# Layer 0 attention: q/k channels stored by groups of four heads

## The reference

```
q, k, v = split_heads(x @ Wq + bq), split_heads(x @ Wk + bk), split_heads(x @ Wv + bv)
pos_k = split(rel_embeddings @ Wk + bk)                # 64 positions x 16 heads x 8
scores = (q k^T + take(q pos_k^T, bucket(i - j)) + take(k pos_k^T, bucket(j - i))^T) / sqrt(24)
ctx = softmax(scores) @ v
x += layernorm(ctx @ Wo + bo + xn) + xn @ sign(weight).T + ...
```

## Time and profile before

| | us |
|---|---|
| median of 3 runs | 2037.45 (2034.83 to 2041.1) |
| profiled execution | 2038.12 |
| its span, first to last instruction | 2036.3 |
| PE busy / VectorE / ScalarE / GpSimd | 1878.0 / 1517.2 / 1475.5 / 1200.4 |
| mean granted TensorE clock | 0.966 |

### The profile page before, as it was taken

The page is one execution under the profiler, slowest core; times in us unless marked ns, Lnnn a source line. Parts: engine busy times, 40 slices in busy tenths (PEclk is TensorE's granted clock), DMA queues, the critical chain, the costliest instruction groups (busy, mean ns, idle before and its releaser), DMA issues.

```text
span 2036.3 us, 38730 instructions
## 1 busy us (share of the span) xinstructions
PE 1878.0 (92%) x13494; PEld 1471.1 (72%) x13494; DVE 1517.2 (75%) x3871; ACT 1475.5 (72%) x2979; POOL 1200.4 (59%) x1027
## 2 busy tenths in 40 slices
PE   4899999999999996789998999999999888889998
PEld 3677777777777774554776888888887666668797
DVE  7677777777787874474488888888889777754686
ACT  6788888888888885334466677777776677775675
POOL 3888889798888873365255555555556444447200
PEclk7999999999999999699998999999999899999999
DMA  6999999999999992101000000000010000012001
GB/s 189 334 337 327 326 332 322 316 338 308 342 314 329 323 327 74 72 1 41 1 6 1 1 1 1 1 1 1 1 33 1 1 1 1 1 47 79 12 1 42
DMA packets 72263, 263.98 MB, mean 130 GB/s; under 512 B 10822, under 2 KB 30406, under 8 KB 71558
## 3 DMA queue, kind: packets, MB, share of 16 engines
q1 hardware_dynamic: 71126, 256.53, 36.6%
q10 hardware_dynamic: 944, 4.98, 0.6%
HBM read 140.17 MB, written 121.31 MB: 128 GB/s over the span
## 4 chain that ended last, share of the span: by engine, by line
PE 42%; DVE 7%; ACT 6%; POOL 2%; issue 1%; DVEq 0%; ACTq 0%; POOLq 0%
PE PS L157 10%; PE PS L339 8%; PE PS L161 8%; PE PS L163 8%; PE PS L162 8%; ACT AR L167 3%; ACT L167 2%; DVE AR L185 1%; DVE DR L181 1%; ACT PT L171 1%; DVE PT L181 1%; POOL AR L176 1%; DVE AR L193 1%; DVE AR L176 1%; DVE AR L181 0%
## 5 line engine op out<-in xcount | busy, mean ns | idle before, releaser
L167 ACT ACTIVATE AR<-PS,AR 128x512 f32<-128x512 f32 x1024 | 702.9, 693 | 164.6 <-PE PS L339 69.6
L339 PE MATMUL PS<-ident,AR 128*128 128x128 f32 x3816 | 581.3, 277 | 29.7 <-DVE PT L181 16.1
L339 PEld LDWEIGHTS PS<-ident,AR 128*128 128x128 f32 x3816 | 445.2, 142 | 122.7 <-issue 41.4
L157 PE MATMUL PS<-AR 128*128 128x128 bf16 (+7 forms) x4126 | 472.2, 357 | 38.1 <-DVE AR L1394 14.1
L181 POOL TENSOR_TENSOR AR<-AR 128x512 f32<-128x512 f32 (+7 forms) x325 | 385.1, 1199 | 184.1 <-DVE AR L181 64.2
L207 DVE CUSTOM_DVE_ANT_0 PS<-PS,AR 128x512 f32<-128x512 f32 x512 | 353.3, 695 | 165.9 <-PE PS L587 162.8
L176 POOL TENSOR_SCALAR AR<-AR 128x512 f32<-128x512 f32 (+1 forms) x146 | 255.9, 1754 | 263.8 <-DVE AR L1798 195.7
L157 PEld LDWEIGHTS PS<-AR 128*128 128x128 bf16 (+4 forms) x4126 | 297.7, 131 | 141.7 <-issue 92.1
L171 ACT ACTIVATE AR<-PS 128x512 f32<-128x512 f32 (+3 forms) x596 | 354.6, 597 | 49.9 <-PE PS L157 27.8
L193 DVE TENSOR_REDUCE AR<-PS 128x1 f32<-128x512 f32 x384 | 263.9, 688 | 82.7 <-PE PS L163 76.1
L171 ACT ACTIVATE PT<-PS 128x512 fp32r<-128x512 f32 x320 | 191.4, 598 | 161.9 <-PE PS L339 127.3
(11 more groups left out here) (177 smaller groups left out, 3070.2 us busy)
## 6 DMA issues: line engine op xcount, KB each, us to landing
scr<-AR SPq DMA_DIRECT2D x128, 800.0 KB, 5.2
XN<-scr SPq DMA_DIRECT2D x85, 768.0 KB, 7.1
AR<-scr SPq DMA_DIRECT2D x43, 768.0 KB, 7.2
AR<-qsc SPq DMA_DIRECT2D x96, 192.0 KB
qsc<-AR SPq DMA_DIRECT2D x16, 384.0 KB, 4.4
qsc<-AR SPq DMA_DIRECT2D x16, 256.0 KB, 4.6
AR<-in_wgu SPq DMA_DIRECT2D x16, 256.0 KB, 3.2
qsc<-AR SPq DMA_DIRECT2D x16, 128.0 KB, 4.9
```

Source lines behind the costliest of these rows:

```text
L157: return pe.e.matmul(out, lhsT, rhs, start=start, stop=stop)
L167: return ac.e.activation(out, in_, func, bias=bias, scale=scale, accum_out=accum)
L339: return pe.e.transpose(out, in_, ident[0:k, 0:k])
```

## The change

Channels are ordered by group of four heads first, then channel-in-head, then head in the group: partition p = 32 g + 4 d + h'. The weights' columns, the biases and `mask16` are reordered with it. In each block of `qsc` a group's 32 rows now lie together, 32 KB. The wide reads get a new source pattern, six blocks of eight runs of 4 KB. For `PGO` the four heads of each group must now be picked apart, so its reads run over four dimensions of 1 KB pieces, and the two that covered 24 partitions at once become three each: 12 DMAs instead of 8.

```diff
--- before.py
+++ after.py
@@ -22,7 +22,9 @@
 
 BACK_D = ROW_D - 64
 BACK = BACK_D + FRAME_D[3] + 192
-QSZ = 2 * 16 * 48 * 512 + 16 * 12 * 512
+QPART = 128 * 512
+QFAR = 2 * 6 * QPART
+QSZ = QFAR + 16 * 12 * 512
 SC = float(1.0 / np.sqrt(np.float32(24.0)))
 
 
@@ -74,12 +76,13 @@
     c["iota"] = np.tile(np.arange(64, dtype=np.float32)[None, :], (128, 1))
     c["rev"] = np.tile(np.arange(8, 0, -1).astype(np.float32)[None, :], (128, 1))
     head = i // 8
+    head_by_channel = 4 * (i // 32) + i % 4
     pat = np.zeros((128, 3), np.float32)
     pat[54:57, 0] = 1
     pat[48:51, 1] = 1
     pat[51:54, 2] = 1
     c["pat"] = pat
-    c["mask16"] = (i[:, None] % 16 == i[None, :16]).astype(np.float32)
+    c["mask16"] = (head_by_channel[:, None] == i[None, :16]).astype(np.float32)
     c["bdmask"] = (head[:, None] == head[None, :]).astype(np.float32)
     return c
 
@@ -625,7 +628,7 @@
             norm_tr(pe, 0, 2, 4, 2)
             norm_tr(pe, 0, 3, 4, 3)
             pe.wait_ge(*emptied[number["g0", 0, 0]])
-            pe.wait_ge(pg_r, 8 * 16)
+            pe.wait_ge(pg_r, 12 * 16)
             pe.wait_ge(dv_init, PV_0)
             for n in range(2):
                 g_of(n, 0)
@@ -1055,13 +1058,12 @@
             sp.wait_ge(po_init, PGO_0)
             for k in range(2):
                 for part, first, step, times in PLACES[1 - k]:
-                    for x in range(first, first + step * times, step if step > 1 else times):
-                        n = times if step == 1 else 1
-                        src = bass.AP(pgd.tensor, (2 * part + k) * 128 * 128, [[0, n], [2048, 8], [1, 2048]])
-                        sp.e.dma_start(flat(PGO[8 * x:8 * (x + n), k]), src).then_inc(pg_r, 16)
+                    for x in range(first, first + step * times, step):
+                        src = bass.AP(pgd.tensor, (2 * part + k) * 128 * 128, [[512, 8], [4096, 4], [1, 512]])
+                        sp.e.dma_start(flat(PGO[8 * x:8 * x + 8, k]), src).then_inc(pg_r, 16)
 
             def q_write(b, k):
-                base = b % 2 * QSZ + k * 16 * 48 * 512
+                base = b % 2 * QSZ + k * 6 * QPART
                 sp.wait_ge(sp_p, 6 * b + 2 * k + 2 if b else SPLIT0[k, 1])
                 sp.wait_ge(sp_a, 6 * b + 2 * k + 2 if b else SPLIT0[k, 1])
                 if b >= 2:
@@ -1074,14 +1076,14 @@
                                    flat(PARTS[2][0:64])).then_inc(qw[b % 2], 16)
                     return
                 for part, first, step, times in PLACES[k]:
-                    dst = bass.AP(qsc.tensor, base + first * 8 * 8192, [[512, 128], [step * 8 * 8192, times], [1, 512]])
+                    dst = bass.AP(qsc.tensor, base + first * QPART, [[512, 128], [step * QPART, times], [1, 512]])
                     sp.e.dma_start(dst, bc(PARTS[k][:, part:part + 1, :], [128, times, 512])).then_inc(qw[b % 2], 16)
 
             def rows(G, k):
-                return bass.AP(qsc.tensor, G // 4 % 2 * QSZ + k * 16 * 48 * 512 + G % 4 * 2048, [[8192, 48], [1, 2048]])
+                return bass.AP(qsc.tensor, G // 4 % 2 * QSZ + k * 6 * QPART + G % 4 * 32 * 512, [[QPART, 6], [2048, 8], [1, 2048]])
 
             def far_rows(G, k, n):
-                at = G // 4 % 2 * QSZ + 2 * 16 * 48 * 512 + (32 * (k // 2) + 8 * (G % 4) + k % 2) * 1536
+                at = G // 4 % 2 * QSZ + QFAR + (32 * (k // 2) + 8 * (G % 4) + k % 2) * 1536
                 return bass.AP(qsc.tensor, at, [[512, n], [3072, 4], [1, 512]])
 
             def load_group(G):
@@ -2908,7 +2910,7 @@
     d = constants()
 
     d["x"] = f["L0_attn_hidden_states"].reshape(NT, 128, 128).transpose(1, 0, 2)
-    by_channel = np.arange(128).reshape(16, 8).T.reshape(128)
+    by_channel = np.arange(128).reshape(4, 4, 8).transpose(0, 2, 1).reshape(128)
     d["l0_wq"], d["l0_wk"] = f["L0_attn_Wq"][:, by_channel], f["L0_attn_Wk"][:, by_channel]
     d["l0_wv"], d["l0_wo"] = f["L0_attn_Wv"], f["L0_attn_Wo"]
     d["l0_sw"] = f["L0_ffn_weight"].T
```

## The result

| | before | after |
|---|---|---|
| median of 9 runs | 2037.58 us (2033.82 to 2041.1) | 2045.12 us (2040.38 to 2047.82) |
| ratio, 95% interval | | 1.0036 [1.0027, 1.0045] |
| profiled execution, span | 2038.1, 2036.3 | 2041.8, 2040.0 |
| mean granted TensorE clock | 0.966 | 0.967 |

The change costs 7.5 us, where 17 were forecast: the likeliest case in kind (slower, with six engines on the wide reads), with its price more than twofold too high. The profiled execution is one of the quicker ones of the changed kernel, 3.3 us under its median. So I took the same kernel's profile once more (run e10_after_again, 2049.55 us) and read both.

A forecast was written before the change was run, and what follows sets the result against it. It took PE as nearly full, 590.2 of 600 us busy, with the DMA engines close behind at share 0.94. Loop lateness 16 plus start 1.3 made 17 us, so 2055 us; range 2036 to 2110.

The forecast's parts named there:

- the likeliest case: Layer 0's attention loop: six engines just full from the wide reads, 2055 us, own range 2044 to 2080; chance 0.52.
- What bounds it: Steady loop: PE busy 590.2 of 600 us, DMA share 0.94; two resources close to full.
- Six engines: Wide reads of `qsc`: outer count falls from 48 to 6, so six engines carry 32 KB each per read.
- the rival that the read is still spread over sixteen: Wide reads: each engine has 20.4 us of work per group; shares the chances of 0.10 (faster) and 0.18 (hidden).
- The work of the fullest engine: Per group in the loop: six engines 22.6 us, lowest three 22.9, in a period of 22.9 us.
- The choice of 3.6 us for six engines against 9.8: Wide reads per group on six engines: 3.6 us at 27.3 GB/s taken, 9.8 us at 10.1 GB/s rejected.
- the rival of slow packets: Wide reads: 4 KB packets stay slow, half of them giving 2137 us, a quarter 2089; chance 0.20 with the mild form.
- a third of it: Loop: a third of the lateness of up to 1.7 us reaches PE, 0.5 us per group, 16 us in all.
- The route: Loop: late `scr` transfers meet GpSimd's wait, then reach `least` on VectorE, then the exponential, then PE.
- Bursts: Head issuing a group's two loads: 7.15 us of work against 5.71, so it falls behind and two heads catch up.
- The slow rate: Early wide reads before the change: 161 GB/s at share 1.00, tied to rows 16 KB apart.
- The start: `PGO` reads: 12 DMAs instead of 8 delay the writes of q and k and the first load, costing 1.3 us.

The follow-up runs named there:

- e10_after_again: The changed kernel with no edit, run again for a second profile: 2044.33 us, ratio 1.0037; its profiled execution 2049.55 us.
- e7: Changed kernel with a group's two wide reads of `load_group` issued four steps apart instead of one behind the other: 2050.11 us, ratio 1.0072.
- e12: Changed kernel with the wide reads issued between a head's write and its read of `scr`, instead of behind the read: 2057.17 us, ratio 1.0095.
- e5: Changed kernel with a group's 48 rows in one piece, read over sixteen engines, each `qsc` write split into four: 2044.87 us, ratio 1.0041.
- the probe: Kernel before, plus six stretches of eight 4 KB-row reads after its output's store, varying row spacing and destination partitions: 2106.32 us including these reads.
- e1: Changed kernel with operand rows ordered channel-in-head first, so wide reads have outer count 8 and use eight engines: 2041.26 us, ratio 1.0024.

## Why the prediction was right or wrong

**What bounds it.** Right. PE remains the bound, busy for 97 to 98% of the steady stretch, and easing the DMA engines brings nothing: no run beats the kernel before.

**Six engines.** Right, and the rival that the read is still spread over sixteen fell with the share of 0.36 and 129 GB/s for a wide read alone. In the steady stretch the GB/s stay while the share falls by 0.03 to 0.04. The rule on engine counts that I took from the Trainium skill, "DMA: Bandwidth & Descriptors", section "Why a DMA increments its semaphore by 16 and not by 1", agrees with the traces here for three and six.

**The work of the fullest engine.** Right where it can be tested. By the same sum eight engines carry 2.7 us of wide reads per group, near the 2.5 taken for before, and the loop stays at 721 us. Three carry 7.2; the sum gives (26.5 - 22.9) x 32 = 115 us, and the loop grew by 104. The choice of 3.6 us for six engines against 9.8 is borne out, and the rival of slow packets in both its forms fell with it.

**The step that failed** is "I let a third of it through to PE, 0.5 us per group: 32 x 0.5 = 16 us". In the two profiles the loop grew by 2.0 and 9.2 us, 0.06 and 0.29 us per group; by the medians (7.5 - 1.0) / 32 = 0.2. The third was no measurement but a guess between none and all. It was set at a place where hardly any lateness goes through: GpSimd's waits grew by half and VectorE saw 0.6 us more. That 41 of 105 heads have a wait there only shows that GpSimd is early; the 0.2 us of VectorE in the earlier trace rows show that none of it was passed on, not how much room is left. I took the cover as used up. It held another 28 us of GpSimd's waits, but for one place at a batch's `tail`. Nor is the price a fraction of every group's lateness: what PE lost, it lost in a few long waits.

**The route.** Wrong in the main. As far as the waits show it, most of the lateness that reaches PE goes through the write of `scr`. It lands at 6.1 instead of 5.2 us, VectorE waits for its buffer 9.5 and 13.3 us instead of 0, and in the second profile PE waits 6.3 us more for VectorE. In the first profile nothing of the 9.5 reaches PE as a wait for VectorE between 100 and 700 us, so for that execution's 2.0 us the route is not shown; the predicted route has 0.59 us of it. Three engines enlarge that route to 83.5 and 51.8 us, while the wait for GpSimd stays at 6.1. In the prediction writes stood beside reads as landing up to 1.7 us later, but I asked for the readers' waits only. Who waits for a write was counted for SyncE alone; before the change no compute engine did. e7 and e12 limit this: with reads a little later still the predicted route becomes the dear one, and it opens at the heads that share GpSimd with a batch's `tail`.

**Bursts.** Not shown. The working let a head with two loads fall behind and two heads catch up; taking the loads apart eased the waits for writes, but late reads met GpSimd's `tail` and the changed kernel became slower. How much the burst itself costs stays open.

**The slow rate.** The number 161 GB/s was read rightly, its cause was not. That "the 16 KB spacing that goes with the slow rate is gone" is refuted as a reason by e5 (170 GB/s with touching rows) and by the probe (154 against 161). It is the 48 neighbouring partitions of the destination, and the change left these alone. The share of 1.00 there was no measure of work: the sixteen engines are counted busy while they are held back. That six engines draw no more than this rate is why they lose nothing on a wide read alone; it was the second of the two reasons given for 3.6 us, and it alone carries. The Trainium skill, "DMA: Bandwidth & Descriptors", section "Latency and other measured facts", ties slow copies to large powers of two in the row spacing; no run here shows that at 16 KB, and the use I made of it as a direction was wrong.

**The start.** The size was right (1.0 to 1.3 us), the working not. 12 issues took 4.10 us and not 5.9, so an issue of rows of 1 KB costs 0.34 us; the mean of 0.49 came from a row that mixes two shapes, two of the eight in the three-dimensional form. The first load went out at 29.32 and not near 30.7. The larger part of the delay comes from this same form in the wide reads, 0.5 and 0.4 us more of the queue each; e1, with the form but eight engines, leaves 0.3 to 0.4 us to the six engines. I read this from the timelines; no run isolates it.

## What to carry to other kernels

Before lateness is passed on to the bottleneck by a fraction, list every buffer whose release hangs on the transfers that get later, the writes' too, and ask of each how far it is from being waited for: a wait of 0 in the trace may be the first to open. An engine that waits longer has cost nothing until the engine behind it waits; read that second wait's row for the size, and look in the timeline at long waits that a view puts under "issue". Look first at the places where an engine with slack has extra work, once in a batch: there the slack runs out. When an access pattern is changed, compare its outer counts on the DMA engines and its issue time in the queue; a lower total share can mean fuller engines.

## What the runs showed of the hardware

- A read from DRAM into 48 neighbouring partitions is held to 154 to 161 GB/s with sixteen engines and 153 with six; 48 rows into every second of 96 partitions reach 298, 128 partitions 402 to 416. Row spacing of 16 KB in DRAM against touching rows changed little: 161 and 154 for 48 partitions, 402 and 416 for 128.
- An engine's busy share counts time in which it is held back: 1.03 at 161 GB/s and 1.02 at 416.
- Issue time on SyncE's queue depends on the form. At the start of the kernel: 0.31 to 0.33 us for 48 rows in two dimensions, 0.66 to 0.84 with the third, 0.34 for 8x4 pieces of 1 KB, and 0.71 where the destination takes every sixth partition (12 in 8.51 us). In the loop the same form varies: the first wide read of a load took 0.91 us at the median in two dimensions (before) and 0.73 in three (after), the second 0.32 and 0.72.
- One kernel's profiled executions can differ by 7.7 us while the median of its runs moves by less than 1 (2045.12 and 2044.33): a reading of a few us needs a second profile.
